# Softmax of a dilated-attention kernel: subtracting the maximum and summing the exponentials on TensorE instead of VectorE

## The chip, the cores and the metric

One core of one Trainium2 chip. The metric is the device time of the kernel in microseconds (us), from its start to its end; the profiled execution has a span beside that time, which is the stretch that the engine records cover.

The engines: TensorE (PE; its weight loads are listed as PEld), VectorE (DVE), ScalarE (ACT), GpSimd (POOL), and SyncE (SP), which only issues transfers here.

## What is computed

The input x is 8 x 128 x 16 x 16 in fp32. Two blocks are added to it in turn:

```python
x = x + _L0_conv_ref(_gn(x), w_qkv, w_gate, b_gate)       # dilated attention, 4 dilations (1, 2, 4, 8), gated
x = x + _L1_conv_ref(_gn(x), W_qkv, b_qkv, W_proj, b_proj)  # attention between channels, 4 heads

# the first block, for each dilation (32 channels, 2 heads of 16)
attn = jnp.einsum('bhdn,bhdkn->bhnk', qh, kp) * scale     # kp: k at the 9 neighbours of each pixel
attn = jax.nn.softmax(attn, axis=-1)                      # over the 9 neighbours
out = jnp.einsum('bhnk,bhdkn->bnhd', attn, vp)
```

The softmax over the nine neighbours is the part that the change touches.

## The kernel before, in words

Everything is on one core, written out by hand: five engine programs with an order of their own each, joined by semaphores. No scheduler moves anything.

The eight images are worked on in two phases of four. Within a phase the partitions hold 4 images x 32 channels, and a free axis of 256 pixels. The first block does, for each phase `ph` and dilation index `s` (0 to 3):

- `project` (PE): one tile per kind (q, k, v) and s, four 32-column matmuls side by side; ScalarE copies each tile out of PSUM (`copy_tile`). Two q tiles of phase 1 stay in PSUM: `project_query` writes them over the scores of phase 0.
- `multiply_qk` (DVE, L572): q times k at the nine neighbours, three calls per s (one per column offset).
- `sum_scores` (PE): sums over the channels of a head with a 0/1 matrix; the scores of the 32 (image, head, s) rows and 9 x 64 pixels of a phase go to PSUM, bank `SC[ph]` and the next, three column offsets 256 apart (`SC = (4, 6)`).
- The softmax: `softmax_shift` (DVE, L579 and L582) takes the maximum over the nine and writes scores minus maximum to `shifted` in SBUF; `softmax_exp` (ACT, L395) takes the exponential into `expd`; `softmax_divide` (DVE, L589, L590, L592) sums the nine, takes the reciprocal, and multiplies by it and by the gate into `prob`.
- `spread` (PE, twelve chunks per phase): spreads a chunk of `prob` over the channels, into one of two PSUM halves in turn; chunk c waits for the product of chunk c - 2.
- `multiply_pv` (DVE, L613): that times v. GpSimd (L340) adds up the neighbours of all of phase 0 and half of phase 1, beginning once the first product is there; VectorE (L625) adds the rest.
- `restore` (PE) brings the sums back to channel order, once all additions of a phase are done, and `first_residual` (DVE, L632) adds x. From there the second normalisation (its reciprocal root on GpSimd, L305) and the second block run, in four groups of two images.

`keep_clock(n)` on PE is n matmuls into an unused bank. Between the phases the engines overlap: in the stretch that the change touches (about 20 to 50 us), VectorE mixes phase 1's `multiply_qk` with phase 0's softmax and `multiply_pv`.

Of the kernel before, what the change touches and what calls it, by code (L numbers as in the profile page):

```python
# [5 lines left out]
P = 128  # L6
# [3 lines left out]
ND = len(DIL)  # L10
# [3 lines left out]
KK = 9  # L14
PHASES = 2
SLOTS = B // PHASES
QP = N // 4
# [7 lines left out]
SCALE0 = float(HD) ** -0.5  # L25
# [16 lines left out]

W_QKV, W_GATE, W_1T, W_PT, W_B1, W_BP, W_BG, W_END = 0, 384, 388, 516, 644, 645, 646, 650

C_ID, C_GRP, C_RED, C_BLK, C_DIL, C_END = 0, 128, 256, 384, 512, 516


def columns(d, ci):
# [43 lines left out]
def view(t, offset, dims, p0=0, parts=P):  # L92

    step = t[:].ap[0][0]
    return bass.AP(t, p0 * step + offset, [[step, parts]] + [list(x) for x in dims if x[1] > 1])


def build(nc, x, wpack, consts, selc, out):
    with ExitStack() as ctx:  # L99
        def sb(name, shape, dtype=F32):  # L100
            return ctx.enter_context(nc.sbuf_tensor(name, shape, dtype))

        def sem(name):
            return ctx.enter_context(nc.semaphore(name))
# [9 lines left out]
        qk = [sb(f"qk{s}", [P, KK, N]) for s in range(ND)]  # L114
        pv = [sb(f"pv{s}", [P, KK, N]) for s in range(ND)]
        acc = sb("acc", [P, PHASES, ND, N])
        shifted = sb("shifted", [P, KK, QP])
        expd = sb("expd", [P, KK, QP])
        prob = sb("prob", [P, PHASES, KK, QP])

        smax = sb("smax", [P, QP])
        ssum = sb("ssum", [P, QP])
        srec = sb("srec", [P, QP])

        sums = sb("sums", [P, B, 2])
# [74 lines left out]
        q_ready = sem("q_ready")  # L200
        qk_ready = sem("qk_ready")
        scores_ready = sem("scores_ready")
        shift_ready = sem("shift_ready")
        exp_ready = sem("exp_ready")
        prob_ready = sem("prob_ready")
        spread_ready = sem("spread_ready")
        pv_ready = sem("pv_ready")
# [141 lines left out]
        def _(act):  # L349
# [41 lines left out]
            def softmax_exp(ph):  # L391
                act.wait_ge(shift_ready, ph + 1)
                if ph:
                    act.wait_ge(prob_ready, ph)
                nc.scalar.activation(expd[:], shifted[:], ACT.Exp, scale=SCALE0).then_inc(exp_ready, 1)  # L395

            def squares(g):

# [46 lines left out]
            for n in range(7, 11):  # L445
                copy_tile(n)
            gate_exp()
            for n in range(11, 18):
                copy_tile(n)
            softmax_exp(0)  # L450
            for n in range(18, len(tiles)):
                copy_tile(n)
            softmax_exp(1)
            squares(0)
# [37 lines left out]
        def _(dve):  # L492
            settled = [0]

            def link(ins):

                settled[0] += 1
                ins.then_inc(dve_settled, 1)
                dve.wait_ge(dve_settled, settled[0])
# [73 lines left out]
                if ci == 2:  # L573
                    last.then_inc(qk_ready, 1)

            def softmax_shift(ph):

                dve.wait_ge(scores_ready, ND * (ph + 1))
                link(nc.vector.tensor_reduce(smax[:], view(ps, 512 * SC[ph], [[1, QP], [256, 3], [QP, 3]]), AX.XY, ALU.max))  # L579
                if ph:  # L580
                    dve.wait_ge(exp_ready, ph)
                nc.vector.tensor_tensor(shifted[:].rearrange("p (c r) n -> p c r n", r=3),  # L582
                                        view(ps, 512 * SC[ph], [[256, 3], [QP, 3], [1, QP]]),
                                        view(smax, 0, [[0, 3], [0, 3], [1, QP]]), ALU.subtract).then_inc(shift_ready, 1)

            def softmax_divide(ph):

                dve.wait_ge(exp_ready, ph + 1)
                link(nc.vector.tensor_reduce(ssum[:], view(expd, 0, [[1, QP], [QP, KK]]), AX.X, ALU.add))  # L589
                link(nc.vector.reciprocal(srec[:], ssum[:]))  # L590
                dve.wait_ge(gate_ready, 1)
                nc.vector.scalar_tensor_tensor(out=prob[:, ph, :, :], in0=expd[:], scalar=gate[:, ph:ph + 1],  # L592
                                               in1=view(srec, 0, [[0, KK], [1, QP]]), op0=ALU.mult, op1=ALU.mult
                                               ).then_inc(prob_ready, 1)
# [93 lines left out]
                multiply_qk(0, 3, i)  # L688
            for i in range(2):
                multiply_qk(1, 0, i)  # L690
            softmax_shift(0)
            multiply_qk(1, 0, 2)
            multiply_qk(1, 1, 0)
            softmax_divide(0)
            for i in range(1, 3):
                multiply_qk(1, 1, i)
            multiply_qk(1, 2, 0)
            for i in range(3):
                multiply_pv(0, 0, i)
            for i in range(1, 3):  # L700
                multiply_qk(1, 2, i)
            for i in range(2):
                multiply_pv(0, 1, i)
            for i in range(3):
                multiply_qk(1, 3, i)
            multiply_pv(0, 1, 2)
            for i in range(3):
                multiply_pv(0, 2, i)
            softmax_shift(1)
            for i in range(2):  # L710
                multiply_pv(0, 3, i)
            softmax_divide(1)
# [48 lines left out]
        def _(pe):  # L761
# [19 lines left out]
            def project(n):  # L781

                kind, s, ph = tiles[n]
                if n == 0:
                    pe.wait_ge(w_loaded, 16)
                bank = PROJ_BANKS[n % len(PROJ_BANKS)]
                if n >= len(PROJ_BANKS):
                    pe.wait_ge(proj_copied, n - len(PROJ_BANKS) + 1)
                w0 = W_QKV + P * kind + CD * s
                for j in range(SLOTS):  # L790
                    b = PHASES * j + ph
                    if n % (3 * ND) == 0:

                        every = [PHASES * i + h for h in range(PHASES) for i in range(SLOTS)]
                        same = [x for x in every if (x in NORM_ON_ACT) == (b in NORM_ON_ACT)]
                        pe.wait_ge(xn_act_ready if b in NORM_ON_ACT else xn_ready, same.index(b) + 1)
                    last = mm(ps[32 * j:32 * j + 32, bank, 0:N], wp[:, w0:w0 + CD], xn[:, b, :])
                last.then_inc(proj_ready, 1)

            def project_query(s):  # L800

                pe.wait_ge(shift_ready, 1)
                for j in range(SLOTS):
                    last = mm(view(ps, q_columns(s), [[1, N]], 32 * j, 32), wp[:, W_QKV + CD * s:W_QKV + CD * s + CD],
                              xn[:, PHASES * j + PHASES - 1, :])
                last.then_inc(q_ready, 1)
# [9 lines left out]
            def sum_scores(ph, s):  # L816
# [22 lines left out]
                        last = mm(o, w, m, start=(s == 0), stop=(s == ND - 1 and ci > 0))  # L839
                last.then_inc(scores_ready, 1)  # L840

            def spread(ph, s, chunk):

                ci = CENTRE_FIRST[chunk]
                c = 12 * ph + 3 * s + chunk
                if c % 12 == 0:
                    pe.wait_ge(prob_ready, ph + 1)
                if c == 0:
                    pe.wait_ge(sel_loaded, 64)
                    pe.wait_ge(proj_copied, len(tiles))  # L850
                if c >= 2:
                    pe.wait_ge(pv_ready, c - 1)
                c0, c1, _ = columns(DIL[s], ci)
                for j in (0, 2, 1, 3):
                    i0, i1 = row_offsets(s, j)
                    dims = lambda slot, row: [[slot, i1 - i0], [row, QR], [1, c1 - c0]]
                    o = view(ps, 1024 * (c % 2) + 64 * QR * j + W * i0 + c0, dims(W, 64))
                    half = 64 * (j // 2)
                    m = view(prob, (ph * KK + 3 * ci + i0) * QP + c0, dims(QP, W), half, 64)
                    last = mm(o, sel[half:half + 64, j % 2, s, :], m)  # L860
                last.then_inc(spread_ready, 1)

            def restore(g):

                ph, first = g // 2, GB * (g % 2)
                if g % 2 == 0:
                    pe.wait_ge(added, ADDS * sum(POOL_SUMS[:ph + 1]))
                    if POOL_SUMS[ph] < ND:
                        pe.wait_ge(dve_added, ADDS * (ND - POOL_SUMS[ph]))
                if ph == 0:  # L870
                    pe.wait_ge(shift_ready, g + 1)
                    pe.wait_ge(qk_ready, ND * PHASES)
                if g == 2:
                    pe.wait_ge(pv_ready, 12 * PHASES)
                for i in range(GB):
                    for s in range(ND):
                        last = mm(ps[32 * s:32 * s + 32, BANK[g] + i, 0:N],
                                  ident[:, 32 * (first + i):32 * (first + i) + 32], acc[:, ph, s, :])
                    last.then_inc(restored, 1)
# [56 lines left out]
            project(14)  # L936
            for i in range(2, 4):
                sum_scores(0, i)
            for n in range(15, 18):
                project(n)  # L940
            for i in range(2, ND):
                project_query(i)
            for n in range(18, len(tiles)):
                project(n)
            sum_scores(1, 0)
            for i in range(2):
# [7 lines left out]
            spread(0, 1, 2)  # L954
            spread(0, 2, 0)
            sum_scores(1, 2)
            keep_clock(1)
            for i in range(1, 3):
                spread(0, 2, i)
            sum_scores(1, 3)  # L960
            for i in range(2):
                spread(0, 3, i)
            keep_clock(2)
            spread(0, 3, 2)
            keep_clock(6)
            for i in range(3):
                spread(1, 0, i)
            spread(1, 1, 0)
# [94 lines left out]
```

## Time and profile before

| | |
|---|---|
| median of 3 runs | 84.35 us (84.25 to 84.52) |
| the profiled execution | 84.39 us, span 82.6 us |
| busy PE / PEld | 67.3 us (81%) / 49.0 us (59%) |
| busy DVE | 69.6 us (84%) |
| busy POOL | 42.4 us (51%) |
| busy ACT | 30.7 us (37%) |
| granted TensorE clock, mean | 1.00 |

How to read it: no engine is busy all the time, and each is waited for at some stage, so a share says little; the chain of waits (followed back from the last instruction) says who sets the time at which stage. The timeline of an engine merges neighbouring instructions of one kind. An fp32 matmul leaves two MATMUL and two LDWEIGHTS records, so "x8" in a PE row is four matmuls. A matmul's record lasts until its result has drained, and overlaps the next one's.

### The profile page before, as it was taken

The numbers are of one execution on the slowest core, as the hardware profiler recorded it, in microseconds if no ns is written. First come the engines' busy times: TensorE is split into PE (matmuls) and PEld (weight loads), VectorE is DVE, ScalarE is ACT, GpSimd is POOL, SyncE is SP. The second block draws the span as 40 slices with busy tenths as digits, with TensorE's granted clock in tenths as the row PEclk, the third lists the DMA queues.
The fourth block names the chain that finished last, engine by engine and source line by source line (L and its number), as shares of the span: only waits on it lengthen the run. The fifth ranks groups of instructions, "written<-read, shape, count | busy, mean of one in ns | idle before, by whom it ended". The sixth has DMA issues, their size and how long they took to land.

```text
span 82.6 us, 2228 instructions
## 1 busy us (share of the span) xinstructions
PE 67.3 (81%) x888; PEld 49.0 (59%) x888; DVE 69.6 (84%) x191; ACT 30.7 (37%) x97; POOL 42.4 (51%) x82
## 2 busy tenths in 40 slices
PE   0099899799867979999966797979999787999960
PEld 0099695476433656686855664667685545677830
DVE  1087679999999999999999698889999999857980
ACT  4396599615537000000030004220993155485320
POOL 7104279108700009999999999899990003300000
PEclk9999999999999999999999999999999999999999
DMA  0995004000000000000000000000000000011244
GB/s 5 315 356 150 1 0 100 5 0 0 8 0 0 4 12 0 0 0 0 12 0 0 0 0 0 0 8 0 0 0 0 0 8 4 0 63 64 71 158 159
DMA packets 3019, 3.11 MB, mean 38 GB/s; under 512 B 320, under 2 KB 2752, under 8 KB 3008
## 3 DMA queue, kind: packets, MB, share of 16 engines
q1 hardware_dynamic: 2576, 2.69, 9.9%
q10 hardware_dynamic: 432, 0.26, 1.4%
q8 instruction: 7, 0.11, 0.6%
q14 instruction: 4, 0.03, 0.1%
HBM read 1.91 MB, written 1.05 MB: 36 GB/s over the span
## 4 chain that ended last, share of the span: by engine, by line
DVE 42%; POOL 29%; PE 13%; issue 5%; DMA 4%; ACT 2%; POOLq 1%; ACTq 0%
DVE qk L572 17%; POOL acc L340 13%; POOL pv L340 12%; PE ps L763 11%; DVE pv L613 5%; DMA xt<-x_dram 4%; POOL rstd L305 4%; DVE acc L625 4%; DVE pv L625 3%; DVE x L632 2%; PE ps L898 2%; DVE ssum L589 1%; ACT pT L402 1%; DVE x L658 1%; POOLq L99 1%
## 5 line engine op out<-in xcount | busy, mean ns | idle before, releaser
L763 PE MATMUL ps<-prob,sel 64*128 64x192 f32 (+6 forms) x192 | 17.7, 313 | 2.9 <-DVE pv L613 1.9
L613 DVE TENSOR_TENSOR pv<-ps,v 128x128 f32<-128x128 f32 (+7 forms) x32 | 17.1, 569 | 1.7 <-PE ps L763 0.9
L763 PE MATMUL ps<-xn,wp 128*32 128x256 f32 (+1 forms) x208 | 16.4, 382 | 1.7 <-DVE shifted L582 1.2
L763 PEld LDWEIGHTS ps<-prob,sel 64*128 64x128 f32 x192 | 13.7, 186 | 6.9 <-DVE pv L613 4.8
L340 POOL TENSOR_TENSOR pv<-pv 128x240 f32<-128x240 f32 (+3 forms) x24 | 14.6, 617 | 0.1
L572 DVE TENSOR_TENSOR qk<-q,k 128x720 f32<-128x720 f32 (+7 forms) x24 | 13.9, 646 | 0.1
L763 PE MATMUL ps<-xt 128*128 128x128 f32 x56 | 10.6, 334 | 4.1 <-DMA xt<-x_dram 4.1
L763 PEld LDWEIGHTS ps<-xn,wp 128*32 128x32 f32 (+1 forms) x208 | 9.7, 116 | 6.3 <-DVE shifted L582 1.7
L340 POOL TENSOR_TENSOR acc<-acc,pv 128x256 f32<-128x256 f32 (+4 forms) x20 | 12.6, 635 | 0.5
L305 POOL TENSOR_TENSOR rstd<-gvar,mhalf 128x2 f32<-128x2 f32 (+1 forms) x6 | 4.9, 824 | 14.9 <-DVE gvar L516 14.9
L763 PEld LDWEIGHTS ps<-xt 128*128 128x128 f32 x56 | 8.6, 230 | 5.2 <-DMA xt<-x_dram 4.1
L763 PE MATMUL ps<-qk,cs 128*32 128x192 f32 (+6 forms) x176 | 7.8, 302 | 0.9 <-ACT v L385 0.5
L340 POOL TENSOR_TENSOR acc<-pv 128x256 f32<-128x256 f32 x4 | 2.9, 728 | 8.5 <-DVE pv L613 8.5
L395 ACT ACTIVATE expd<-shifted 128x576 f32<-128x576 f32 x2 | 1.4, 684 | 15.8 <-DVE shifted L582 15.8
L402 ACT ACTIVATE pT<-x 128x256 f32<-128x256 f32 x8 | 3.3, 411 | 10.4 <-DVE x L632 10.4
L763 PEld LDWEIGHTS ps<-qk,cs 128*32 128x32 f32 x176 | 4.7, 109 | 3.6 <-ACT v L385 1.0
L541 DVE TENSOR_REDUCE sums<-xt 128x1 f32<-128x256 f32 x8 | 2.8, 413 | 2.8 <-DMA xt<-x_dram 2.8
L763 PE MATMUL ps<-p,mT 128*128 128x256 f32 x16 | 4.6, 399 | 0.3 <-ACT mT L429 0.2
L763 PE MATMUL ps<-acc,cs 128*32 128x256 f32 x64 | 4.1, 383 | 0.7 <-issue 0.6
L360 ACT ACTIVATE xn<-xt 128x256 f32<-128x256 f32 x8 | 3.2, 404 | 2.0 <-DMA xt<-x_dram 2.0
L415 ACT ACTIVATE p<-ps,wp 128x256 f32<-128x256 f32 x8 | 3.4, 473 | 1.1 <-PE ps L763 1.1
L572 DVE TENSOR_TENSOR qk<-ps,k 128x128 f32<-128x128 f32 (+4 forms) x12 | 3.8, 379 | 0.0
(75 smaller groups left out, 94.0 us busy)
## 6 DMA issues: line engine op xcount, KB each, us to landing
xt<-x_dram SPq DMA_DIRECT2D x4, 256.0 KB, 3.6
out_dram<-x SPq DMA_DIRECT2D x8, 128.0 KB, 1.8
wp<-wpack_dram SPq DMA_DIRECT2D x1, 325.0 KB, 5.6
sel<-selc_dram SPq DMA_DIRECT2D x4, 64.0 KB, 3.9
cs<-consts_dram ACTq DMA_DIRECT2D x1, 130.0 KB, 3.3
cs<-consts_dram ACTq DMA_DIRECT2D x2, 64.0 KB, 2.6
```

What stands on the lines that cost most here:

```text
L305: nc.gpsimd.tensor_tensor(rstd[:, bs], gvar[:, bs], mhalf[:, bs], ALU.pow).then_inc(rstd_ready, 1)
L340: nc.gpsimd.tensor_tensor(o, a, b, ALU.add).then_inc(added, 1)
L360: nc.scalar.activation(xn1[:, b // GB, b % GB, :], xt[:, b, :], ACT.Square, accum_out=sums[:, b, 1:2]).then_inc(square_ready, 1)
L402: nc.scalar.activation(pT[:, g, 2 * i:2 * i + 2, :].rearrange("p t n -> p (t n)"), x1[:, b, :], ACT.Square, accum_out=sums1[:, b, 1:2]).th ...
L415: nc.scalar.activation(p1[:, g, i, :], ps[:, BANK[g] + i, 0:N], ACT.Identity, bias=wp[:, W_B1:W_B1 + 1]).then_inc(p1_copied, 1)
L541: nc.vector.tensor_reduce(sums[:, b, 0:1], xt[:, b, :], AX.X, ALU.add).then_inc(sum_ready, 1)
L572: last = nc.vector.tensor_tensor(o, a, b, ALU.mult)
L613: last = nc.vector.tensor_tensor(o, a, b, ALU.mult)
L625: nc.vector.tensor_tensor(o, a, b, ALU.add).then_inc(dve_added, 1)
L632: nc.vector.scalar_tensor_tensor(out=x1[:, b, :], in0=ps[:, BANK[g] + i, 0:N], scalar=1.0, in1=xt[:, b, :], op0=ALU.mult, op1=ALU.add, acc ...
L763: return nc.tensor.matmul(o, w, m, start=start, stop=stop)
L898: last = nc.tensor.transpose(ps[:, BANK[g] + i, P * t:P * t + P], p1[:, g, i, P * t:P * t + P], ident)
```

## The change

- The subtraction on VectorE goes. `softmax_max` keeps the maximum; `shift_scores` on TensorE adds minus the maximum onto the scores in PSUM, by two matmuls with a negated identity (384 and 192 columns). ScalarE's exponential reads PSUM. The buffer `shifted` goes.
- The sum of the nine exponentials on VectorE goes. `sum_exponentials` on TensorE does it by nine accumulating matmuls of 64 columns with the identity as weights, into the bank behind the scores; the reciprocal reads PSUM.
- `project_query` (both) and phase 0's `restore` calls (both) wait for later events (the exponential, the probabilities), since they write over what is read then.
- The table of constants gets 128 columns more (the negated identity), in the second load of them.
- The orders on DVE, PE and ACT change to match, and three `keep_clock` calls lose four matmuls in all (1 + 2 + 6 becomes 5).

```diff
-C_ID, C_GRP, C_RED, C_BLK, C_DIL, C_END = 0, 128, 256, 384, 512, 516
+C_ID, C_GRP, C_RED, C_BLK, C_DIL, C_NEG, C_END = 0, 128, 256, 384, 512, 516, 644
...
-                nc.scalar.activation(expd[:], shifted[:], ACT.Exp, scale=SCALE0).then_inc(exp_ready, 1)
+                nc.scalar.activation(expd[:].rearrange("p (c r) n -> p c (r n)", r=3),
+                                     view(ps, 512 * SC[ph], [[256, 3], [1, 3 * QP]]), ACT.Exp, scale=SCALE0).then_inc(exp_ready, 1)
...
-            def softmax_shift(ph):
+            def softmax_max(ph):
 
                 dve.wait_ge(scores_ready, ND * (ph + 1))
-                link(nc.vector.tensor_reduce(smax[:], view(ps, 512 * SC[ph], [[1, QP], [256, 3], [QP, 3]]), AX.XY, ALU.max))
                 if ph:
-                    dve.wait_ge(exp_ready, ph)
-                nc.vector.tensor_tensor(shifted[:].rearrange("p (c r) n -> p c r n", r=3),
-                                        view(ps, 512 * SC[ph], [[256, 3], [QP, 3], [1, QP]]),
-                                        view(smax, 0, [[0, 3], [0, 3], [1, QP]]), ALU.subtract).then_inc(shift_ready, 1)
+                    dve.wait_ge(shift_ready, ph)
+                nc.vector.tensor_reduce(smax[:], view(ps, 512 * SC[ph], [[1, QP], [256, 3], [QP, 3]]), AX.XY,
+                                        ALU.max).then_inc(max_ready, 1)
 
             def softmax_divide(ph):
 
-                dve.wait_ge(exp_ready, ph + 1)
-                link(nc.vector.tensor_reduce(ssum[:], view(expd, 0, [[1, QP], [QP, KK]]), AX.X, ALU.add))
-                link(nc.vector.reciprocal(srec[:], ssum[:]))
+                dve.wait_ge(ssum_ready, ph + 1)
+                link(nc.vector.reciprocal(srec[:], ps[:, SC[ph] + 1, 0:QP]))
...
-                pe.wait_ge(shift_ready, 1)
+                pe.wait_ge(exp_ready, 1)
...
+            def shift_scores(ph):
+
+                pe.wait_ge(max_ready, ph + 1)
+                for first, n in ((0, 2), (2, 1)):
+                    last = nc.tensor.matmul(view(ps, 512 * SC[ph] + 256 * first, [[256, n], [1, 3 * QP]]), cs[:, C_NEG:C_NEG + P],
+                              view(smax, 0, [[0, n], [0, 3], [1, QP]]), start=False, stop=True, skip_group_check=True)
+                last.then_inc(shift_ready, 1)
+
+            def sum_exponentials(ph):
+
+                pe.wait_ge(exp_ready, ph + 1)
+                for slot in range(KK):
+                    last = mm(ps[:, SC[ph] + 1, 0:QP], ident, expd[:, slot, :], start=(slot == 0), stop=(slot == KK - 1))
+                last.then_inc(ssum_ready, 1)
...
-            for n in range(15, 18):
+            for n in range(15, 17):
                 project(n)
+            shift_scores(0)
+            for n in range(17, 20):
+                project(n)
+            sum_exponentials(0)
             for i in range(2, ND):
                 project_query(i)
-            for n in range(18, len(tiles)):
+            for n in range(20, len(tiles)):
                 project(n)
```

TensorE's program, phase 0's softmax. In the rows, `xn,wp` are the projections (four matmuls a tile), `qk,cs` the scores, `prob,sel` the spreads, `smax,cs` the shift and `expd,cs` the sum. Before, from the last scores of phase 0:

```order
L763 MATMUL ps<-qk,cs 32x8x8 x4
L763 MATMUL ps<-xn,wp 32x256 x36
L763 MATMUL ps<-qk,cs 32x2x192 x4
L763 MATMUL ps<-qk,cs 32x192 x4
L763 MATMUL ps<-prob,sel 128x3x4x16 x4
```

The same place in the change:

```order
L760 MATMUL ps<-qk,cs 32x8x8 x4
L760 MATMUL ps<-xn,wp 32x256 x8
L843 MATMUL ps<-smax,cs 128x2x192
L843 MATMUL ps<-smax,cs 128x192
L760 MATMUL ps<-xn,wp 32x256 x12
L760 MATMUL ps<-expd,cs 128x64 x9
L760 MATMUL ps<-xn,wp 32x256 x16
L760 MATMUL ps<-qk,cs 32x2x192 x4
L760 MATMUL ps<-qk,cs 32x192 x4
L760 MATMUL ps<-prob,sel 128x3x4x16 x4
```

The nine projection tiles are the same; the shift stands behind the second and the sum behind the fifth, so both stand ahead of phase 1's first scores and of the first spread.

TensorE's program in phase 1's softmax, in the change (the rows `prob,sel` are spreads of phase 0, s = 2 and 3):

```order
L760 MATMUL ps<-qk,cs 32x8x8 x4
L760 MATMUL ps<-prob,sel 128x2x4x12
L760 MATMUL ps<-prob,sel 128x3x4x12 x2
L760 MATMUL ps<-prob,sel 128x2x4x12
L843 MATMUL ps<-smax,cs 128x2x192
L843 MATMUL ps<-smax,cs 128x192
L760 MATMUL ps<-prob,sel 128x2x4x12
L760 MATMUL ps<-prob,sel 128x3x4x12 x2
L760 MATMUL ps<-prob,sel 128x2x4x12
L760 MATMUL ps<-prob,sel 128x2x4x16 x4
L760 MATMUL ps<-expd,cs 128x64 x9
L760 MATMUL ps<-prob,sel 128x2x4x8 x8
```

Before, both spreads of s = 2 that are left and the first two of s = 3 ran without such rows between them; now the shift stands in front of two spreads and the sum in front of the last two.

VectorE's program in the change, from phase 0's reciprocal to the first products with v:

```order
L588 RECIPROCAL srec<-ps 128x64 [waits ssum_ready]
L590 SCALAR_TENSOR_TENSOR prob<-expd,gate,srec 128x576 [waits gate_ready,dve_settled]
L573 TENSOR_TENSOR qk<-ps,k 128x16x12 [waits q_ready,scores_ready,proj_copied]
L573 TENSOR_TENSOR qk<-ps,k 128x2x12x12
L573 TENSOR_TENSOR qk<-ps,k 128x256
L573 TENSOR_TENSOR qk<-ps,k 128x2x192
L573 TENSOR_TENSOR qk<-ps,k 128x16x12
L573 TENSOR_TENSOR qk<-ps,k 128x2x12x12
L611 TENSOR_TENSOR pv<-ps,v 128x768 [waits spread_ready,proj_copied]
```

Before, the products of s = 1 (two calls of `multiply_qk`) and one of the three of s = 2 stood between `prob` and the first product with v, and the other two of s = 2 came after three products with v. Now s = 1 is done ahead of the reciprocal, and all three of s = 2 stand behind `prob`.

## Rows read from the trace of the kernel before

**Rows 1.** Chain of waits, in order of time (start us, us, what), 48 to 51 us

```profile
48.80 0.47 POOL acc L340
...
49.31 0.96 DVE pv L613
50.27 0.35 DVE x L632 x2
```

**Rows 2.** Timeline of DVE, 21.9 to 33 us (start us, us, engine line op out<-in)

```profile
21.93 0.75 DVE L579 TENSOR_REDUCE smax<-ps 128x64 f32<-128x576 f32 x1
22.71 0.76 DVE L582 TENSOR_TENSOR shifted<-ps,smax 128x576 f32<-128x576 f32 x1
23.38 1.67 DVE L572 TENSOR_TENSOR qk<-q,k 128x720 f32<-128x720 f32 x2
24.96 1.23 DVE L589 TENSOR_REDUCE ssum<-expd 128x64 f32<-128x576 f32 x1
26.22 0.55 DVE L590 RECIPROCAL srec<-ssum 128x64 f32<-128x64 f32 x1
26.81 0.82 DVE L592 SCALAR_TENSOR_TENSOR prob<-expd,gate,srec 128x576 f32<-128x576 f32 x1
...
29.18 0.71 DVE L572 TENSOR_TENSOR qk<-ps,k 128x192 f32<-128x192 f32 x2
29.82 1.76 DVE L613 TENSOR_TENSOR pv<-ps,v 128x768 f32<-128x768 f32 x2
...
32.57 1.51 DVE L572 TENSOR_TENSOR qk<-ps,k 128x256 f32<-128x256 f32 x4
```

**Rows 3.** Timeline of PE, 20 to 32 us; idle before and releaser in brackets

```profile
23.52 2.80 PE L763 MATMUL ps<-xn,wp 128*32 128x256 f32 x48 [1.20 <-DVE shifted L582]
26.81 1.18 PE L763 MATMUL ps<-qk,cs 128*32 128x384 f32 x16 [0.49 <-ACT v L385]
27.91 1.53 PE L763 MATMUL ps<-prob,sel 64*128 64x192 f32 x16
29.38 0.94 PE L763 MATMUL ps<-xt 128*128 128x128 f32 x6
30.82 1.41 PE L763 MATMUL ps<-prob,sel 64*128 64x180 f32 x12 [0.51 <-DVE pv L613]
```

**Rows 4.** Timeline of ACT, phase 0's exponential

```profile
23.50 0.69 ACT L395 ACTIVATE expd<-shifted 128x576 f32<-128x576 f32 x1 [0.74 <-DVE shifted L582]
```

**Rows 5.** Timelines of PEld and PE: short matmuls behind 128-column weight loads

```profile
14.76 0.52 PEld L763 LDWEIGHTS ps<-wp,pexp 128*128 128x128 f32 x4 [0.71 <-POOL pexp L317]
...
14.76 0.61 PE L763 MATMUL ps<-wp,pexp 128*128 128x4 f32 x4 [0.23 <-POOL pexp L317]
...
42.46 0.66 PE L763 MATMUL ps<-prob,sel 64*128 64x64 f32 x8 [0.69 <-DVE pv L613]
```

**Rows 6.** Timeline of PE, two rows of 33 to 46 us

```profile
32.71 0.84 PE L763 MATMUL ps<-prob,sel 64*128 64x168 f32 x8 [0.16 <-DVE pv L613]
...
40.02 1.11 PE L763 MATMUL ps<-prob,sel 64*128 64x128 f32 x16
```

**Rows 7.** Timeline of DVE, phase 1's probabilities

```profile
44.49 0.89 DVE L592 SCALAR_TENSOR_TENSOR prob<-expd,gate,srec 128x576 f32<-128x576 f32 x1
```

**Rows 8.** Timeline of POOL: the first addition, and the first wait after it

```profile
30.84 0.73 POOL L340 TENSOR_TENSOR acc<-pv 128x256 f32<-128x256 f32 x1 [8.51 <-DVE pv L613]
...
52.90 0.71 POOL L305 TENSOR_TENSOR rstd<-gvar,mhalf 128x2 f32<-128x2 f32 x1 [0.29 <-DVE gvar L516]
```

**Rows 9.** DMA issues of the constants: KB each, median us from issue to landing

```profile
cs<-consts_dram ACTq DMA_DIRECT2D x1, 130.0 KB, 3.3
cs<-consts_dram ACTq DMA_DIRECT2D x2, 64.0 KB, 2.6
```

**Rows 10.** Timeline of PE: phase 0's first scores, and its last

```profile
15.65 1.18 PE L763 MATMUL ps<-qk,cs 128*32 128x384 f32 x16 [0.28 <-DMA cs<-consts_dram]
...
19.27 1.75 PE L763 MATMUL ps<-qk,cs 128*32 128x96 f32 x48
```

More of the change, by code:

```diff
@@ L121, in build @@
         smax = sb("smax", [P, QP])
-        ssum = sb("ssum", [P, QP])
         srec = sb("srec", [P, QP])
@@ L202, in build @@
         scores_ready = sem("scores_ready")
+        max_ready = sem("max_ready")
         shift_ready = sem("shift_ready")
         exp_ready = sem("exp_ready")
+        ssum_ready = sem("ssum_ready")
         prob_ready = sem("prob_ready")
@@ L447, in _ @@
             gate_exp()
-            for n in range(11, 18):
+            for n in range(11, 17):
                 copy_tile(n)
             softmax_exp(0)
-            for n in range(18, len(tiles)):
+            for n in range(17, len(tiles)):
                 copy_tile(n)
@@ L690, in _ @@
                 multiply_qk(1, 0, i)
-            softmax_shift(0)
+            softmax_max(0)
             multiply_qk(1, 0, 2)
-            multiply_qk(1, 1, 0)
+            for i in range(3):
+                multiply_qk(1, 1, i)
             softmax_divide(0)
-            for i in range(1, 3):
-                multiply_qk(1, 1, i)
-            multiply_qk(1, 2, 0)
+            for i in range(3):
+                multiply_qk(1, 2, i)
             for i in range(3):
                 multiply_pv(0, 0, i)
-            for i in range(1, 3):
-                multiply_qk(1, 2, i)
             for i in range(2):
@@ L706, in _ @@
             multiply_pv(0, 1, 2)
-            for i in range(3):
+            multiply_pv(0, 2, 0)
+            softmax_max(1)
+            for i in range(1, 3):
                 multiply_pv(0, 2, i)
-            softmax_shift(1)
             for i in range(2):
@@ L870, in restore @@
                 if ph == 0:
-                    pe.wait_ge(shift_ready, g + 1)
+                    pe.wait_ge(prob_ready, g + 1)
                     pe.wait_ge(qk_ready, ND * PHASES)
@@ L938, in _ @@
                 sum_scores(0, i)
-            for n in range(15, 18):
+            for n in range(15, 17):
                 project(n)
+            shift_scores(0)
+            for n in range(17, 20):
+                project(n)
+            sum_exponentials(0)
             for i in range(2, ND):
                 project_query(i)
-            for n in range(18, len(tiles)):
+            for n in range(20, len(tiles)):
                 project(n)
@@ L956, in _ @@
             sum_scores(1, 2)
-            keep_clock(1)
+            sum_scores(1, 3)
+            spread(0, 2, 1)
+            shift_scores(1)
+            spread(0, 2, 2)
+            spread(0, 3, 0)
+            sum_exponentials(1)
             for i in range(1, 3):
-                spread(0, 2, i)
-            sum_scores(1, 3)
-            for i in range(2):
                 spread(0, 3, i)
-            keep_clock(2)
-            spread(0, 3, 2)
-            keep_clock(6)
+            keep_clock(5)
             for i in range(3):
@@ L1049 @@
         (p[:, None] // HD1 == p // HD1).astype(np.float32),
-        (p[:, None] % 32 // 8 == np.arange(ND)).astype(np.float32)], axis=1)
+        (p[:, None] % 32 // 8 == np.arange(ND)).astype(np.float32), -np.eye(P, dtype=np.float32)], axis=1)
     selc = np.zeros((32, ND, P), np.float32)
```

1 line of the change is left out of this document (removed).

## The prediction

> **What bounds the kernel now.** I read the chain of waits first. Between 31 and 49 us it lies on GpSimd, whose additions of phase 0 end at 48.80 + 0.47 = 49.27; then VectorE's product (49.31, 0.96) and the residual at 50.27 [rows 1]. The reader is to see that two paths meet there. GpSimd starts at 30.84 with the first product and waits for nothing noteworthy until 52.90 [rows 8]; its end plus a restored tile (about 0.65, what one tile costs when the six of 2.80 us start 0.43 apart [rows 3]) and two hops of 0.05 would allow the residual at 50.0, so this path has only 0.2 us to spare. The other one leaves phase 1's probabilities at 44.49 + 0.89 = 45.38 [rows 7] and gets, by spreads and products in turn, to the residual 4.9 us later [rows 1]. Behind the residual nothing is changed, and GpSimd itself waits there for VectorE's variance (0.29 at 52.90 [rows 8]), so a delay of the residual moves the end in full. The question is therefore when the first product with v starts (29.82 now [rows 2]), and when phase 1's probabilities end.
>
> Next the timelines of VectorE, TensorE and ScalarE at phase 0's softmax. VectorE runs there with no gap from 21.93 to the products [rows 2]: it sets the time, and TensorE follows with waits of 1.20 and 0.49 [rows 3].
>
> **What is removed.** On VectorE two subtractions (0.76 each) and two sums (1.23 each, less 0.08 that an instruction overlaps the next) [rows 2]: 3.9 us of its time. On TensorE four `keep_clock` matmuls; three of them take 0.94 with about 0.2 of draining [rows 3], so 0.25 each. The one of them that stands in the way is the one between phase 0's spreads; the others fall into waits.
>
> **What is added.** The shift: 384 + 192 columns in one full-width tile. The scores' group has the same columns in four tiles side by side and takes 1.18, with the next group 1.10 behind its start [rows 3]. I take 1.15 until it lands and 1.05 until the next matmul. The shapes' widths differ, so the bounds are 0.9 and 1.3.
>
> The sum: nine fp32 matmuls of 64 columns, each with its own loads of 128 weight columns, two records a matmul. No row of before has this shape. Rows near it: four matmul records of 4 columns take 0.61 behind four loads that take 0.52 [rows 5]; one load alone is 0.19 of that, so loads follow each other every 0.11. And a spread of 64 columns, whose eight loads go four each to two row halves, still takes 0.66 [rows 5], hardly less than the 1.11 / 2 of the 128- and 64-column pair [rows 6]. Streaming is cheaper: 0.25 for a matmul of 128 columns is 0.12 a record, so 0.06 for 64. The loads bound it: 18 x 0.11 = 2.0 us, landing 0.2 later. Lower bound: only the streams count, 18 x 0.06 = 1.0. Upper bound: load and stream don't overlap, 18 x 0.17 = 3.0. I take 2.0, since loads of this width are in the rows at 0.11. The Trainium skill (page "TensorE: Matmul & The Clock Gate", section "Back-to-back issue gap") gives a matmul of 1 to 64 columns about 60 cycles, some 25 ns, with no word of its loads in that table; by it the sum would cost 0.45 us, and the time would be about 84.3. The 4-column rows at 0.11 a record speak against it.
>
> The exponential from PSUM: 0.69 [rows 4] either way; it ends at 23.9 + 0.7 = 24.6, ahead of where TensorE gets to the sum, so it costs nothing in phase 0. The reciprocal from PSUM: taken at 0.55 as now.
>
> **Phase 0, step by step.** The maximum ends at 22.67 [rows 2]. TensorE starts the shift at 22.72 (it has finished its two tiles by then), and goes on at 23.77; three tiles at 0.43: 25.06; the sum: 27.06, landed at 27.25; two queries and two tiles, 4 x 0.43: 28.78, landed 28.98; then ScalarE's last copy and the hops, 0.49 as now: 29.47; phase 1's first scores, 1.10: 30.57; the first spread, about 0.97 (more than half of the pair's 1.53 [rows 3]): the first product can start at **31.54**, against 29.82: **+1.7**.
>
> VectorE meanwhile: four products (twice the pair's 1.67 [rows 2]) end at 25.9, then it idles until 27.3 for the sum; reciprocal 0.59 and probabilities 0.74 with their gaps; `multiply_qk` of s = 2, 0.71 + 1.51 less overlaps [rows 2]: 30.6. It idles again, for 0.9. So the 1.9 us that left VectorE here are waited away, and TensorE is the bound. GpSimd starts 1.7 later, ends at 51.0, and allows the residual at 51.7.
>
> **Phase 1.** From the first spread (27.91 [rows 3]) to the landing of the second spread of s = 3 (40.02 + 1.11 = 41.13 [rows 6]) TensorE needs 13.2 us, of it waits of 0.51 and 0.16 [rows 3, 6], which vanish now that TensorE is the late one. Less these and the 0.25 of `keep_clock`, plus the shift's 1.05 and the sum's 2.0, it is 15.35: from 30.57 to 45.9. The sum stands ahead of this spread, and VectorE's program has the product of this spread ahead of the reciprocal. Product 0.4 (two short ones), reciprocal 0.59, probabilities 0.85: they end at 47.75, against 45.38: +2.4; small waits of TensorE that I can't list one by one may give back 0.2. So the residual is at about **+2.3**, and GpSimd's path, at +1.5 (1.7 less its 0.2 to spare), is covered by it. In this stretch too VectorE waits (for scores, for spreads) longer than the 1.9 us that it saves.
>
> **Other edits.** The second load of constants grows from 130 to 194 KB. Twice 64 KB cost 2.6 to 3.3 us to landing [rows 9], so some 0.7 for 64 KB more; phase 0's first scores already wait 0.28 for it [rows 10]. The last scores of phase 0 would land at 21.0 + 0.7 = 21.7, and VectorE comes to the maximum at 21.93 by itself [rows 10, 2]: nothing, with 0.2 left; if the load came a microsecond late, 0.8 would be added. The later waits of `project_query` and `restore` cost nothing: the exponential is over before the sum, which stands ahead on the same queue.
>
> **Sum.** 84.39 of the profiled execution + 2.3 = **86.7**; the median is 84.35, 0.04 off, which changes nothing. Each 1 us of the sum's price counts nearly twice, once in each phase, so the forecast's own range is 86.0 to 87.4.
>
> **The rivals.**
> 1. *Loads are hidden, the sum costs its streams, 1.0.* Then TensorE reaches the first spread at 29.57 and the first product starts at +0.7; phase 1's path is at +0.3, and GpSimd's binds with 0.7 - 0.2 = +0.5: 84.9. For it: the weights are the same nine times over. Against: every matmul of the page has its loads, and the 4-column rows. The table of the Trainium skill named above (page "TensorE: Matmul & The Clock Gate", section "Back-to-back issue gap") goes further in this direction and would end at no change.
> 2. *Faster: the pair of products on TensorE stays under VectorE's cover.* The place is the first product with v. Without the removed work VectorE alone could start it at 22.6 + 3.2 + 0.6 + 0.7 + 2.1 = 29.2, 0.6 earlier, and GpSimd's chain would follow: 83.8. It decides by the price of shift plus sum: TensorE's path gives 28.5 + price, so below 0.7 VectorE sets the time, at 1.3 it is as now, and I have 3.05. For it: 3.9 us less on the engine that is busiest. Against: the rows of loads and streams, which would have to be wrong by more than half.
> 3. *Load and stream in turn, 3.0*: 2 x 1.0 more, 88.6. Against: three `keep_clock` matmuls with loads of 0.11 and streams of 0.12 take 0.94, not 1.4 [rows 3].
> 4. *It doesn't do what it says, in time:* smaller waits take up both prices, no change, 84.4; or something slower that I don't see, such as the constants' load.
>
> **Chances.** Forecast 0.62, rival 1 0.13, rival 2 0.08, rival 3 0.07, no change 0.05, slower otherwise 0.05. A measurement can tell 0.3% from no change. Faster 0.08; within 0.3% (up to 84.6) 0.05 and a quarter of rival 1: 0.08; slower 0.84. The range 84.8 to 87.9 leaves out rival 2, rival 3 and no change, 0.2 in all.
>
> **What would show it.** Right: nine `expd,cs` matmuls lasting about 2.2 us in each phase, loads every 0.11; VectorE idle over 1 us ahead of phase 0's reciprocal, released by TensorE; the first addition on GpSimd near 32.5; the residual near 52.5; the chain of waits on PE between 23 and 31 us. Wrong: the sum under 1.2 us (rival 1), GpSimd's first addition before 30.8 (rival 2), or VectorE without gaps between 22 and 46 us.

## The result, and the profile after

The change makes the kernel slower: 87.09 us (median of 4 runs, 87.03 to 87.39) against 84.44 us of the kernel before in the same set. The ratio is 1.032 (95% interval 1.029 to 1.036), so 2.7 us. The prediction said slower, 86.7 us. In this document executions that are more than 1.5% above the fastest of their kernel are left out of the ratios (three of 12 in e7, two of seven in e8, four of six in e9), and the profiled executions of e8 and e9 are among those left out, though what makes them longer lies ahead of the mark that the distances below are measured from.

The profiled execution took 87.39 us, with a span of 85.6. It was 0.5 us later than that of before at the start of phase 0's maximum (22.45 against 21.93 [rows 2]). Its chain of waits begins with a later one of the four input transfers, issued at 1.75 us and landed after 4.91, where that of before begins with the first, issued at 0.74 and landed after 3.27. The wider table of constants is not the reason: e11 below, which has it too, starts this maximum at 21.76. So I compare distances from one mark, the start of phase 0's maximum.

The page of the changed kernel: span, busy shares, and what the products with v (L611) waited for.

```profile
span 85.6 us, 2296 instructions
...
PE 72.1 (84%) x924; PEld 53.9 (63%) x924; DVE 65.9 (77%) x187; ACT 30.7 (36%) x97; POOL 42.4 (49%) x82
...
DVE 38%; PE 35%; POOL 8%; DMA 6%; issue 5%; ACT 4%; SPq 1%; POOLq 1%; ACTq 0%
...
L611 DVE TENSOR_TENSOR pv<-ps,v 128x128 f32<-128x128 f32 (+7 forms) x32 | 17.1, 569 | 5.9 <-PE ps L760 5.1
```

The chain's line and the products' line on the page of the kernel before:

```profile
DVE 42%; POOL 29%; PE 13%; issue 5%; DMA 4%; ACT 2%; POOLq 1%; ACTq 0%
...
L613 DVE TENSOR_TENSOR pv<-ps,v 128x128 f32<-128x128 f32 (+7 forms) x32 | 17.1, 569 | 1.7 <-PE ps L763 0.9
```

VectorE has 3.7 us less (69.6 before; the forecast was 3.9), and TensorE 4.8 more (67.3 before). The chain went from VectorE and GpSimd (42% and 29%) to TensorE: 13% before, 35% now. The products with v, which are the same ones as before, now wait 5.1 us for TensorE instead of 0.9.

The chain of waits of the changed kernel, in order of time (start us, us, what):

```profile
22.45 0.76 DVE smax L582
...
23.25 1.24 PE ps L843 x4
24.49 5.49 PE ps L760 x74
...
30.00 0.38 ACT v L385
...
30.43 4.34 PE ps L760 x46
...
35.75 5.04 PE ps L760 x78
...
40.81 0.77 DVE smax L582
...
41.63 1.24 PE ps L843 x4
42.86 3.88 PE ps L760 x40
...
47.76 0.84 DVE prob L590
```

From 23 to 47 us it is TensorE with short breaks, where before VectorE (to 31 us) and GpSimd (to 49) stood.

TensorE's timeline of the changed kernel, phase 0's softmax and the first spread, and phase 1's:

```profile
23.25 1.24 PE L843 MATMUL ps<-smax,cs 128*128 128x384 f32 x4 [0.74 <-DVE smax L582]
24.42 1.50 PE L760 MATMUL ps<-xn,wp 128*32 128x256 f32 x24
25.85 2.22 PE L760 MATMUL ps<-expd,cs 128*128 128x64 f32 x18
28.00 1.93 PE L760 MATMUL ps<-xn,wp 128*32 128x256 f32 x32
30.43 1.18 PE L760 MATMUL ps<-qk,cs 128*32 128x384 f32 x16 [0.49 <-ACT v L385]
31.54 1.53 PE L760 MATMUL ps<-prob,sel 64*128 64x192 f32 x16
...
43.91 2.22 PE L760 MATMUL ps<-expd,cs 128*128 128x64 f32 x18
```

Row by row this is the sum of the prediction: shift, three tiles, sum, four tiles, ScalarE's copy (0.49 as before), scores, spread. VectorE's timeline of the changed kernel:

```profile
28.11 0.56 DVE L588 RECIPROCAL srec<-ps 128x64 f32<-128x64 f32 x1 [1.69 <-PE ps L760]
...
32.57 1.77 DVE L611 TENSOR_TENSOR pv<-ps,v 128x768 f32<-128x768 f32 x2 [0.99 <-PE ps L760]
...
43.58 0.72 DVE L611 TENSOR_TENSOR pv<-ps,v 128x192 f32<-128x192 f32 x2 [1.38 <-PE ps L760]
...
46.77 0.49 DVE L611 TENSOR_TENSOR pv<-ps,v 128x128 f32<-128x128 f32 x2 [1.80 <-PE ps L760]
...
47.76 0.83 DVE L590 SCALAR_TENSOR_TENSOR prob<-expd,gate,srec 128x576 f32<-128x576 f32 x1
...
53.39 0.41 DVE L630 SCALAR_TENSOR_TENSOR x<-ps,xt 128x256 f32<-128x256 f32 x1
```

It waits 1.69 ahead of the reciprocal, 0.99 ahead of the first product, 1.38 and 1.80 in phase 1. From the maximum to the residual it is 53.39 - 22.45 = 30.94 us. In the kernel before, VectorE's timeline has the first residual here:

```profile
50.18 0.41 DVE L632 SCALAR_TENSOR_TENSOR x<-ps,xt 128x256 f32<-128x256 f32 x1
```

That is 50.18 - 21.93 = 28.25, so the change's is longer by **2.69**, the whole loss. GpSimd starts later but is no longer what the residual waits for:

```profile
33.61 0.73 POOL L340 TENSOR_TENSOR acc<-pv 128x256 f32<-128x256 f32 x1 [10.76 <-DVE pv L611]
...
51.46 0.46 POOL L340 TENSOR_TENSOR acc<-acc,pv 128x128 f32<-128x128 f32 x1
...
55.92 0.71 POOL L305 TENSOR_TENSOR rstd<-gvar,mhalf 128x2 f32<-128x2 f32 x1 [0.65 <-DVE gvar L517]
```

Its additions of phase 0 end at 51.92, and at 55.92 it waits 0.65 for VectorE's variance, where it waited 0.29 before [rows 8].

### The profile page after: what moved, and what is told of

It reads as the page before. It is cut to its first block, busy times and chain, and to the rows that moved or that the text cites. A ratio compares the mean times of both kernels' runs of the same rounds, so it can differ in the third digit from the quotient of the medians.

```text
span 85.6 us, 2296 instructions
## 1 busy us (share of the span) xinstructions
PE 72.1 (84%) x924; PEld 53.9 (63%) x924; DVE 65.9 (77%) x187; ACT 30.7 (36%) x97; POOL 42.4 (49%) x82
## 3 DMA queue, kind: packets, MB, share of 16 engines
q1 hardware_dynamic: 2576, 2.69, 9.4%
HBM read 1.97 MB, written 1.05 MB: 35 GB/s over the span
## 4 chain that ended last, share of the span: by engine, by line
DVE 38%; PE 35%; POOL 8%; DMA 6%; issue 5%; ACT 4%; SPq 1%; POOLq 1%; ACTq 0%
PE ps L760 30%; DVE qk L573 11%; DVE pv L611 7%; DMA xt<-x_dram 6%; POOL rstd L305 4%; DVE acc L623 3%; PE ps L843 3%; DVE pv L623 3%; POOL acc L340 3%; DVE x L630 2%; DVE smax L582 2%; POOL pv L340 2%; PE ps L910 1%; DVE x L656 1%; ACT pT L403 1%
## 5 line engine op out<-in xcount | busy, mean ns | idle before, releaser
L611 DVE TENSOR_TENSOR pv<-ps,v 128x128 f32<-128x128 f32 (+7 forms) x32 | 17.1, 569 | 5.9 <-PE ps L760 5.1
L760 PE MATMUL ps<-prob,sel 64*128 64x192 f32 (+6 forms) x192 | 17.1, 311 | 1.0 <-DVE pv L611 0.9
L340 POOL TENSOR_TENSOR pv<-pv 128x240 f32<-128x240 f32 (+3 forms) x24 | 14.1, 597 | 0.1
L760 PE MATMUL ps<-xt 128*128 128x128 f32 x48 | 9.5, 349 | 4.0 <-DMA xt<-x_dram 4.0
L760 PEld LDWEIGHTS ps<-xt 128*128 128x128 f32 x48 | 7.8, 243 | 4.9 <-DMA xt<-x_dram 4.0
L395 ACT ACTIVATE expd<-ps 128x576 f32<-128x576 f32 x2 | 1.3, 653 | 14.1 <-PE ps L843 14.1
L760 PEld LDWEIGHTS ps<-expd,cs 128*128 128x128 f32 x36 | 4.2, 192 | 0.5 <-issue 0.4
L760 PE MATMUL ps<-expd,cs 128*128 128x64 f32 x36 | 4.4, 278 | 0.0
```

The lines of the kernel that those rows point to most:

```text
L340: nc.gpsimd.tensor_tensor(o, a, b, ALU.add).then_inc(added, 1)
L611: last = nc.vector.tensor_tensor(o, a, b, ALU.mult)
L760: return nc.tensor.matmul(o, w, m, start=start, stop=stop)
```

## The experiments

"Path" below is the time from the start of phase 0's maximum to the start of the first residual in the profiled execution: 28.25 us in the kernel before, 30.94 in the change. It leaves out what differs between executions ahead of it and behind it. The theories: *work* (the two steps' own time in TensorE's queue is the loss), *hand-off* (round trips between engines), *order* (VectorE's new order).

**e1: the sum back on VectorE, the shift still on TensorE.**

```diff
-                dve.wait_ge(ssum_ready, ph + 1)
-                link(nc.vector.reciprocal(srec[:], ps[:, SC[ph] + 1, 0:QP]))
+                dve.wait_ge(exp_ready, ph + 1)
+                link(nc.vector.tensor_reduce(ssum[:], view(expd, 0, [[1, QP], [QP, KK]]), AX.X, ALU.add))
+                link(nc.vector.reciprocal(srec[:], ssum[:]))
...
-            sum_exponentials(0)
...
-            sum_exponentials(1)
```

> The change with only the sum of the exponentials put back on VectorE (shift stays on TensorE, orders stay). Work theory (TensorE's own time for the two new steps, in its queue, sets the end): the sum's 2.15 us leave TensorE's path in both phases; VectorE gets 1.2 back in each and sets the first product at about +0.6 against before, GpSimd behind it +0.5: 85.0 us. Hand-off theory (the round trips between engines and the new orders cost the time, however long the matmuls are): one of the two round trips goes, about half of the loss, 85.8. Order theory (the new order of VectorE's products costs it): no gain, 87.1 or more.

Measured: median 85.81, ratio 1.0115 of before (1.003 to 1.020), path 51.35 - 22.50 = 28.85, +0.60. The path is what the work theory gave. The time by itself does not decide: the kernel before had a median of 84.9 in this set of runs, and 1.0115 times the 84.4 that the forecasts start from is 85.4, between the work theory's 85.0 and the hand-off theory's 85.8. Half of the path's 0.60 may lie in one instruction, phase 1's probabilities, which took 1.17 us here and 0.89 before.

**e2: the subtraction back on VectorE, the sum still on TensorE.**

```diff
-                nc.vector.tensor_reduce(smax[:], view(ps, 512 * SC[ph], [[1, QP], [256, 3], [QP, 3]]), AX.XY,
-                                        ALU.max).then_inc(max_ready, 1)
+                link(nc.vector.tensor_reduce(smax[:], view(ps, 512 * SC[ph], [[1, QP], [256, 3], [QP, 3]]), AX.XY, ALU.max))
+                if ph:
+                    dve.wait_ge(exp_ready, ph)
+                nc.vector.tensor_tensor(shifted[:].rearrange("p (c r) n -> p c r n", r=3),
+                                        view(ps, 512 * SC[ph], [[256, 3], [QP, 3], [1, QP]]),
+                                        view(smax, 0, [[0, 3], [0, 3], [1, QP]]), ALU.subtract).then_inc(shift_ready, 1)
...
-            shift_scores(0)
...
-            shift_scores(1)
```

> The change with only the subtraction put back on VectorE (sum stays on TensorE). Work theory: the shift's 1.17 us leave TensorE's path, the sum's 2.15 stay; first product about +1.1, phase 1's probabilities +1.4 against before: 85.8 us, so undoing the shift gains less than undoing the sum. Hand-off theory: each round trip costs alike, also 85.8, and the same as the run without the sum. Order theory: 87.1.

(The exponential reads `shifted` again; those lines are left out here.) Measured: median 86.49 where both theories had 85.8, ratio 1.023 (1.017 to 1.029), path 52.02 - 22.19 = 29.83, +1.58, where the work theory had +1.4. So of the change's 2.69, undoing the sum gives back 2.1 of path and undoing the shift 1.1. That speaks against equal prices for the two round trips, as the hand-off theory wants, but it rests on one profiled execution each, and the intervals of the two ratios overlap; e3, e4 and e9 decide it.

**e3: the same sum as narrow matmuls.**

```diff
                 for slot in range(KK):
-                    last = mm(ps[:, SC[ph] + 1, 0:QP], ident, expd[:, slot, :], start=(slot == 0), stop=(slot == KK - 1))
+                    for j in range(4):
+                        last = mm(ps[32 * j:32 * j + 32, SC[ph] + 1, 0:QP], ident[:, 32 * j:32 * j + 32], expd[:, slot, :],
+                                  start=(slot == 0), stop=(slot == KK - 1))
```

> The change with each of the nine summing matmuls cut into four of 32 weight columns side by side, same sum, same places in all queues. Work theory with the loads as the price: four narrow loads overlap, the sum takes about 1.1 us instead of 2.2; the first product +0.9, GpSimd's path binds at +0.8: 85.2 us. If the sum's price were its hand-offs or a fixed latency, the sum's stretch stays above 2 us and the time at 87.1.

Measured: ratio 1.0165 (1.010 to 1.024), path 51.51 - 22.42 = 29.09, +0.84; the median is 85.87 where 85.2 was expected, in a set of runs in which the kernel before had a median of 84.9 itself. TensorE's timeline of this kernel:

```profile
25.71 1.19 PE L760 MATMUL ps<-expd,cs 128*32 128x64 f32 x72
...
50.81 1.07 PE L760 MATMUL ps<-acc,cs 128*32 128x256 f32 x16 [0.69 <-POOL acc L340]
```

Four times as many matmuls take 1.19 us instead of 2.22, in the same places, with the same hand-offs. And now the restoring matmuls wait 0.69 for GpSimd: its path binds again, as expected. Hand-off and order are the same as in the change, so neither can be the 1.85 us that went. No run has the change's orders with both steps back on VectorE, so how the 0.84 that is left divides between the shift and the orders stays open.

The weight loads of the sum, in the change and then here:

```profile
25.85 2.08 PEld L760 LDWEIGHTS ps<-expd,cs 128*128 128x128 f32 x18 [0.41 <-issue]
```

```profile
25.49 1.24 PEld L760 LDWEIGHTS ps<-expd,cs 128*32 128x32 f32 x72
```

In the change the first 128-column load comes 0.41 behind the last 32-column load of the tiles; here the loads follow on. The three tiles ahead of the sum take 25.71 - 24.39 = 1.32 until the sum begins, and 25.85 - 24.42 = 1.43 in the change: the switch from narrow to wide costs 0.11 at this place.

**e4: the sum twice over.** It accumulates 18 matmuls instead of nine, so its probabilities are half of the reference's.

```diff
-                for slot in range(KK):
-                    last = mm(ps[:, SC[ph] + 1, 0:QP], ident, expd[:, slot, :], start=(slot == 0), stop=(slot == KK - 1))
+                for n in range(2 * KK):
+                    last = mm(ps[:, SC[ph] + 1, 0:QP], ident, expd[:, n % KK, :], start=(n == 0), stop=(n == 2 * KK - 1))
```

> The change with the nine summing matmuls issued twice over (18; the sum is doubled, so the probabilities are half of the reference's). Work theory: 2.0 us more in each phase on the path of TensorE, all of it on the path: 91.1 us. Hand-off or order theory: the matmuls lie beside other work at least in part, well under 89.

Measured: ratio 1.083 (1.075 to 1.090), median 91.62, path 56.86 - 21.80 = 35.06, +6.81.

```profile
25.20 4.23 PE L760 MATMUL ps<-expd,cs 128*128 128x64 f32 x36
```

The sum lasts 4.23, 2.01 longer; the path grew by 6.81 - 2.69 = 4.1, twice that. Nothing hides it in either phase. It also gives the unit price: 18 more pairs of load and matmul record take 2.01, 0.112 each.

**e5: twice the streamed columns behind the same loads.** It leaves slot 8 out of the sum and takes slot 7 twice.

```diff
-                    last = mm(ps[:, SC[ph] + 1, 0:QP], ident, expd[:, slot, :], start=(slot == 0), stop=(slot == KK - 1))
+                    last = mm(ps[:, SC[ph] + 1, 0:2 * QP], ident, expd[:, min(slot, 7):min(slot, 7) + 2, :].rearrange("p a n -> p (a n)"), start=(slot == 0), stop=(slot == KK - 1))
```

> The change with each of the nine summing matmuls streaming 128 columns instead of 64 (two exponentials side by side; the first 64 columns read afterwards hold slots 0 to 7 and slot 7 once more instead of slot 8, so the sum leaves slot 8 out and takes slot 7 twice). If loads of 128 weight columns every 0.11 us are the price, twice the streamed columns are nearly free: the sum's stretch goes from 2.22 us to about 2.3, the time stays at that of the change (about 87.1, within 0.3). If streams count beside loads (load, then stream), the stretch grows by 9 x 0.11 = 1 us and the time by 2 us.

Measured: ratio 1.032 (1.028 to 1.037), the change's own, path 53.12 - 22.08 = 31.04, +2.79.

```profile
25.48 2.27 PE L760 MATMUL ps<-expd,cs 128*128 128x128 f32 x18
```

Doubling the columns costs 0.05 us of 2.22. The price of the sum is its weight loads, and they do overlap with streams (load and stream in turn would have added 1 us a phase).

**e6 and e11: the wide table of constants alone, on the kernel before, twice; e10: a control, with one buffer renamed.**

```diff
-C_ID, C_GRP, C_RED, C_BLK, C_DIL, C_END = 0, 128, 256, 384, 512, 516
+C_ID, C_GRP, C_RED, C_BLK, C_DIL, C_NEG, C_END = 0, 128, 256, 384, 512, 516, 644
```

> The kernel before with only the table of constants made as wide as in the change (194 instead of 130 KB in its second load; nothing reads the new columns). Forecast of the prediction: hidden, ratio 1.000 within 0.3%; phase 0's first scores wait about 0.7 instead of 0.3 us. Rival: the late constants are part of the loss, 0.3 to 0.5 us, ratio 1.004 or more.

> The kernel before with one buffer renamed, nothing else: ratio 1.000; what it shows beside that is what a comparison of this kind adds by itself.

> The kernel before with the wide table of constants once more. If the 0.4% of the first run with it is an effect of the constants, it is 1.003 to 1.005 again and above the renamed kernel in the same set of runs; if not, it is at 1.000 with the renamed one.

Measured: e6 1.0039 (1.0015 to 1.0063), which looked like a miss of the prediction's "nothing". So it was run again beside the control: e11 0.9995 (0.996 to 1.003), e10 1.0004 (0.997 to 1.004). The path is 28.25 in e6 and in e11, as before. The 0.4% didn't come back; the two intervals overlap between 1.0015 and 1.003, so a cost of 0.2% or so is not excluded, and none is shown.

**e7: a new order alone, on the kernel before** (and four `keep_clock` matmuls fewer). The idea comes from the trace: TensorE waited 1.20 for the subtraction and 0.49 for the copies [rows 3], and two queries that are needed late stood early.

```diff
-            for n in range(15, 18):
-                project(n)
-            for i in range(2, ND):
-                project_query(i)
-            for n in range(18, len(tiles)):
+            for n in range(15, len(tiles)):
                 project(n)
             sum_scores(1, 0)
             for i in range(2):
                 spread(0, 0, i)
-            keep_clock(3)
+            for i in range(2, ND):
+                project_query(i)
             spread(0, 0, 2)
...
-            multiply_qk(1, 2, 0)
-            for i in range(3):
+            for i in range(2):
                 multiply_pv(0, 0, i)
+            multiply_qk(1, 2, 0)
+            multiply_pv(0, 0, 2)
```

> The kernel before with a new order alone and all softmax work where it was: all projections ahead of TensorE's wait, the two queries behind the first two spreads, one product of s = 2 behind two products with v. VectorE sets the first product now; it comes 0.6 us earlier, GpSimd's path would allow -0.6, but phase 1's probabilities gain only 0.2 to 0.3 on VectorE's path: ratio about 0.997. Rival: nothing on VectorE's queue got shorter, so 1.000.

Measured: 0.996 (0.992 to 1.000), path 49.93 - 21.91 = 28.02, -0.23. The first product starts 29.12 - 21.91 = 7.21 us behind the maximum instead of 7.89. As expected, but hardly beyond the measurement.

**e8: that order with the narrow sum on TensorE, the subtraction on VectorE.** To e7 it adds, in phase 0, `sum_exponentials(0)` ahead of `sum_scores(1, 0)`, in phase 1 the same ahead of the last spread, in the place of two `keep_clock` matmuls, and the body of e3.

> That order, with the sum of the exponentials on TensorE as four 32-column matmuls side by side for each of the nine (1.15 us), and the subtraction left on VectorE. Work theory: VectorE loses 1.2 us in each phase and TensorE has room for 1.15 in what were waits: first product -1.2, phase 1's probabilities -1.0, ratio about 0.988 of before (83.4 us). Hand-off theory: the extra round trip to TensorE eats it, 1.00.

Measured: **0.988** (0.985 to 0.992), path 51.31 - 23.88 = 27.43, -0.82. This beats both kernels. VectorE's timeline of it, with the maxima, the reciprocals and the residual:

```profile
23.88 0.75 DVE L579 TENSOR_REDUCE smax<-ps 128x64 f32<-128x576 f32 x1
...
27.48 0.56 DVE L589 RECIPROCAL srec<-ps 128x64 f32<-128x64 f32 x1 [0.48 <-PE ps L763]
...
30.45 1.76 DVE L612 TENSOR_TENSOR pv<-ps,v 128x768 f32<-128x768 f32 x2
...
44.79 0.56 DVE L589 RECIPROCAL srec<-ps 128x64 f32<-128x64 f32 x1 [0.99 <-PE ps L763]
...
51.31 0.41 DVE L631 SCALAR_TENSOR_TENSOR x<-ps,xt 128x256 f32<-128x256 f32 x1
```

The first product comes 6.57 us behind the maximum (7.89 before) with no wait in front of it: the extra hand-off to TensorE is there, and the kernel is faster all the same. Of the 1.2%, the order alone is some 0.4% (e7).

**e9: e8 with the sum as nine wide matmuls again**, as in the change.

> The kernel of the run with the new order and the narrow sum, with one thing put back: the sum as nine matmuls with 128-column loads, as in the change. Work theory: the sum's stretch goes from 1.2 to 2.2 us, each time on the path; the time goes from 0.988 of before to about 1.01 (85.4 us). If the order alone made that version fast, it stays under 0.995.

Measured: 1.015 (1.006 to 1.024, from two executions), where 1.01 was forecast; path 52.86 - 23.31 = 29.55, +1.30. From e8 to e9 only the shape of the sum differs: 2.22 instead of 1.2 us on TensorE, 2.1 us of path, 2.7% of the time.

**e12: both steps on TensorE with the narrow sum, in e8's order** (the shift behind the projections of tile 19, in phase 1 behind the last scores).

> Both steps of the change on TensorE (shift as in the change, sum as four 32-column matmuls side by side), in the order of the fast version. Work theory: the shift takes 1.17 us of TensorE and of the path where VectorE's subtraction takes 0.76, so it loses some 0.4 in each phase to that version and more to waits: about 0.2 us above before, ratio 1.002 (1.002 to 1.008 with the wider constants). Rival: VectorE's 3.9 us less pay once the sum is cheap, ratio 0.985 or below.

Measured: 1.0077 (1.0045 to 1.0109), path 51.32 - 22.30 = 29.02, +0.77. Slower than before as the work theory has it, but by 0.5 to 0.6 us more than the 0.2 that I gave; the 1.008 at the end of my range was for wider constants that cost something, which is not shown. TensorE's timeline of this kernel shows a wait of 0.92 ahead of phase 1's shift:

```profile
41.32 1.24 PE L845 MATMUL ps<-smax,cs 128*128 128x384 f32 x4 [0.92 <-DVE smax L582]
```

Work queued behind the shift stands still meanwhile. How the loss divides between this and VectorE's waits was not tried. Against e8, with the subtraction on TensorE (and two tiles behind it), the path is 1.6 us longer, though VectorE has 1.5 us less to do.

## Why the prediction was right

The direction, the mechanism and most of the size were right. The residual was forecast 2.3 later and came 2.69 later, and the time follows it: 87.09 instead of 86.7. Step by step, from the mark at the maximum:

- *What binds.* Right: in phase 0 TensorE's queue between the maximum and the first spread, in phase 1 its queue again; the residual is delayed, and everything behind it in full. The changed kernel's chain and e4 (each microsecond of the sum counts twice) show it.
- *The shift.* Sized 1.05 until the next matmul and 1.15 until it lands; it took 24.42 - 23.25 = 1.17, and 1.24. Mis-sized by 0.1, inside the bounds.
- *The sum.* Sized 2.0 until the next matmul; it took 28.00 - 25.85 = 2.15, and 2.22 until it landed. The bound by loads every 0.11 is shown by e3 (narrow loads: 1.19), e4 (0.112 for each further pair) and e5 (twice the columns: 2.27). So the unit price was right, and the 0.15 that is missing is paid once for the group, not by each record. The figure of the Trainium skill (page "TensorE: Matmul & The Clock Gate", section "Back-to-back issue gap") for a matmul of 1 to 64 columns, about 60 cycles or some 25 ns, is far from it: 2.15 / 18 = 0.12 us here. But that table is for an isolated matmul, and the same section says that in a stream of loads and matmuls both set the spacing, so the prediction's 0.45 applies the table to a case that the section treats apart from it. The page's section "LDWEIGHTS (loading the stationary operand)" gives columns / 1.2 in ns, so 107 ns for 128, and fits: 18 x 0.107 = 1.93, an estimate by that page, against 2.01 for 18 pairs in e4. One reading of rows in the prediction is wrong and carried nothing: the spread of 64 columns takes 0.66, which is more than 1.11 / 2 and not "hardly less".
- *The tiles.* Three took 25.85 - 24.42 = 1.43 instead of 1.29; four and ScalarE's copy 30.43 - 28.00 = 2.43 as forecast (2.41); scores and spread 0.07 more than forecast. Shift, three tiles and sum, each short by 0.12 to 0.15, make most of the 0.5 by which the first product was later than forecast: 32.57 - 22.45 = 10.12 against 7.89, +2.2 instead of +1.7. All three stand where the width of the matmuls changes (128 columns, 32, 128, 32), and my unit prices came from groups of one width. For the tiles ahead of the sum e3 shows it: with a narrow sum behind them they take 1.32, 0.11 less. For the shift and the sum, the change of width as the cause is argued, not shown.
- *VectorE's waits.* 1.69 ahead of the reciprocal (1.4 forecast) and 0.99 ahead of the first product (0.9). Right.
- *Phase 1.* The probabilities ended 48.59 - 22.45 = 26.14 behind the mark, against 23.45: +2.7, where I had +2.4. The first product was 0.5 later than forecast and this only 0.3; which waits of TensorE in between gave the 0.2 back was not read row by row.
- *GpSimd.* Forecast as covered by the other path: shown, it starts 2.2 later than before from the mark (1.7 forecast, short like the first product), and the restoring matmuls don't wait for it.
- *Constants, exponential from PSUM, later waits.* Taken at nothing: the exponential took 0.65 and ended ahead of the sum, a cost of the constants is not shown (e6, e11). They landed after 3.7 us instead of 3.3, 0.4 more where the forecast had 0.7, and phase 0's first scores waited 0.71 for them instead of 0.28 [rows 10]; e10, with the narrow table, waited 0.69 in its profiled execution, so this wait is no measure of the table.

Of the rivals, 1 (cheap sum, 1.0) and 3 (load and stream in turn, 3.0) fell by the first trace, where the sum takes 2.22, and by e5; 2 (under VectorE's cover) fell by the first trace, and 4 (small waits take it up) by e4. Rival 3's time should read 88.7: 86.7 + 2 x 1.0. The hand-off theory, which I added for the experiments, fell by e3, e8 and e9.

## What to carry to other kernels

Relief for the busiest engine is worth only what the engine that takes the work over can hide; look at which queue the new steps enter, and add up that queue between the two events that bound it. Where few columns move behind each weight load, price the loads: with an identity of 128 columns, nine sums of 64 columns took 2.2 us, and cut into four narrow matmuls side by side 1.2, which turned the kernel from 1.5% slower than before into 1.2% faster (e9 and e8). When a step is moved between engines, move also what stands in its way in the queue: here four projections went ahead of the wait and two queries behind the first spreads.

## What the runs showed of the hardware that I had not expected

- In some executions the early projections on TensorE run at about half the pace, though the page lists the granted clock as 1.00 there. Groups of matmuls by shape, 10 to 14 us, of e8's profiled execution and then of the kernel before:

```profile
L763 PE MATMUL ps<-xn,wp 128*32 128x256 f32 x40 | 4.5, 604 | 0.0
```

```profile
L763 PE MATMUL ps<-xn,wp 128*32 128x256 f32 x80 | 4.7, 380 | 0.0
```

  In e10, whose program is that of before, the 88 records of these projections take 7.00 us instead of 5.52; phase 0's maximum starts 0.8 later (22.71) and the execution takes 85.16 us instead of 84.39, with the same path. So it is much of the spread between the profiled executions. What decides it was not tried; it is the reason for measuring from a mark behind it.
- Phase 1's probabilities (576 elements, the same instruction) took 0.83 us on VectorE in the change, 0.89 in the kernel before [rows 7], 1.06 in e8 and 1.17 in e1, each time while GpSimd was adding. In phase 0, ahead of GpSimd's first addition, it took 0.82 in all of these. Why it varies was not tried.
